# Half loads of A with a ScalarE copy, and B 0 by DMA: a change to a recommender tower in float32

## What is computed

```python
for W in Ws:                       # W0 (24*24, 64), W1 (24*64, 64), W2 (24*64, 64)
    H_prev = Xk.shape[1]
    Wr = W.reshape(F_, H_prev, W.shape[1])
    Xk = jnp.einsum('bfd,bhd,fho->bod', X0, Xk, Wr)
    outs.append(Xk.sum(axis=2))
...
h = jnp.concatenate([z, dense_ctx], axis=1)
h = jnp.maximum(h @ W_top1 + b_top1, 0.0)
h = jnp.maximum(h @ W_top2 + b_top2, 0.0)
y = h @ W_top3
```

## Time and profile before

| | us |
|---|---|
| median of 3 runs | 378.74 (377.19 to 379.49) |
| the profiled execution | 375.55 |
| its span, first to last instruction | 373.7 |
| TensorE busy | 353.9 (95%) |
| VectorE busy | 307.8 (82%) |
| ScalarE busy | 187.4 (50%) |
| GpSimd busy | 220.0 (59%) |
| mean granted TensorE clock | 0.991 |

### The profile page before, as it was taken

One profiled execution on the slowest core, in us unless ns is written; L12 is line 12 of the kernel. 1 busy time (PEld: TensorE's weight loads), 2 busy tenths in 40 slices (PEclk: granted clock), 3 DMA queues, 4 the chain that ended last, 5 costly groups with the idle time before them and its releaser, 6 DMA issues.

```text
span 373.7 us, 7214 instructions
## 1 busy us (share of the span) xinstructions
PE 353.9 (95%) x2754; PEld 160.2 (43%) x2754; DVE 307.8 (82%) x308; ACT 187.4 (50%) x352; POOL 220.0 (59%) x332
## 2 busy tenths in 40 slices
PE   0958999999999999999999999999999999999997
PEld 0736623322333345434343454444443444444475
DVE  2993399969897999979898999798999999997600
ACT  1112024146352667574747475837474676545564
POOL 5888888888887878888863888888840000000000
PEclk9978999999999999999999999999999999999999
DMA  7686998979989799989999799979996999540000
GB/s 205 217 160 147 230 165 193 231 166 214 232 196 247 149 232 257 247 178 226 237 241 247 171 254 264 256 147 248 270 251 139 239 257 257 145 139 0 3 2 2
DMA packets 56773, 71.55 MB, mean 191 GB/s; under 512 B 31041, under 2 KB 35777, under 8 KB 56738
## 3 DMA queue, kind: packets, MB, share of 16 engines
q1 hardware_dynamic: 49282, 69.56, 77.8%
q0 software_dynamic: 5376, 1.39, 3.6%
q10 hardware_dynamic: 2080, 0.13, 0.4%
HBM read 50.61 MB, written 1.58 MB: 140 GB/s over the span
## 4 chain that ended last, share of the span: by engine, by line
PE 88%; DVE 7%; ACT 2%; DMA 1%; issue 1%; SPq 0%; DVEq 0%; ACTq 0%
PE ps_x L436 55%; PE ps_b L436 10%; PE ps_tower L436 10%; PE ps_turn L436 7%; DVE Z L373 4%; PE ps_turn L492 3%; PE ps_tower L442 2%; PE ps_turn L500 2%; DMA small_ids_sb<-small_ids 1%; DVE Z L412 1%; ACT x_diag L729 1%; DVE small_ids_f L368 1%; DVE Z L402 1%; DVE x_diag L381 0%; ACT C L702 0%
## 5 line engine op out<-in xcount | busy, mean ns | idle before, releaser
L412 DVE TENSOR_TENSOR Z<-A,ps_b 128x1024 f32<-128x1024 f32 x192 | 221.0, 1213 | 9.8 <-PE ps_x L436 5.5
L230 POOL DMA_INDIRECT x_rows<-tbl,ids_sb x168 | 179.4, 1068 | 55.1 <-POOL pause_sb L241 30.6
L436 PE MATMUL ps_x<-Z,w_sb 128*64 128x512 f32 x768 | 184.2, 598 | 0.7 <-DVE Z L412 0.5
L436 PEld LDWEIGHTS ps_x<-Z,w_sb 128*64 128x64 f32 x768 | 49.3, 136 | 79.9 <-issue 56.1
L402 DVE TENSOR_TENSOR Z<-A,C 128x1024 f32<-128x1024 f32 x48 | 57.6, 1220 | 25.2 <-PE ps_x L436 8.8
L729 ACT ACTIVATE x_diag<-ps_turn,mask_sb 128x192 f32<-128x192 f32 x128 | 50.6, 607 | 14.6 <-PE ps_turn L500 14.6
L436 PE MATMUL ps_x<-Z,w0s_sb 128*64 128x512 f32 x192 | 45.2, 597 | 0.5 <-DVE Z L402 0.3
L241 POOL MEMSET pause_sb<- 128x144 f32 x160 | 40.4, 252 | 0.1
L712 ACT COPY ps_b<-B_sb 128x1024 f32<-128x1024 f32 x36 | 36.9, 1025 | 4.4 <-DMA B_sb<-x_sb 4.0
L742 ACT COPY G<-ps_turn 128x416 f32<-128x416 f32 x31 | 15.7, 505 | 46.7 <-PE ps_turn L436 45.6
L436 PEld LDWEIGHTS ps_turn<-x_diag,x_rows 128*64 128x64 f32 x496 | 25.2, 137 | 17.7 <-issue 17.7
(11 more groups left out here) (60 smaller groups left out, 184.9 us busy)
## 6 DMA issues: line engine op xcount, KB each, us to landing
A<-x_scratch SPq DMA_DIRECT2D x48, 512.0 KB, 11.9
B_sb<-x_sb SPq DMA_DIRECT2D x72, 256.0 KB
C<-x_scratch SPq DMA_DIRECT2D x32, 512.0 KB, 13.2
x_rows<-tbl,ids_sb POOLq DMA_INDIRECT x168
small_ids_sb<-small_ids SPq DMA_DIRECT2D x3, 512.0 KB, 6.1
x_quarters<-x_scratch SPq DMA_DIRECT2D x16, 96.0 KB
x_scratch<-x_rows SPq DMA_DIRECT2D x7, 192.0 KB
w_sb<-w SPq DMA_DIRECT2D x2, 384.0 KB, 5.2
```

The lines of the kernel that those rows point to most:

```text
L230: pool.indirect_dma_start(out=x0_rows[t % 2][:, f * D:(f + 1) * D], out_offset=None, in_=tables[f], in_offset=bass.IndirectOffsetOnAxis(ap ...
L412: nc.vector.tensor_tensor(Z[s % ZR][:, :], A[u % AS][i][:, :], ps_b[j % 2][:, :], ALU.mult)\
L436: return nc.tensor.matmul(out, lhsT, rhs, start=start, stop=stop)
```

## The change

From unit 4 on:

- A's loads write partitions 0 to 63 only (8 repeats instead of 16, 256 KB each), and a new copy_a on ScalarE copies each to partitions 64 to 127. copy_a(u+2) stands in slot u behind copy_c(u+2). It waits for the load and for the last reader of the set. cross1 waits for copy_a instead of the load.
- TensorE no longer makes B 0. SyncE spreads it from x1 (load_b0, two transfers of 256 KB, ahead of load_b) into B0_sb, a buffer that the first part of the kernel used for something else (small_ids_f32[0]), and VectorE reads it from there. B0_sb is single: the load waits until the three products of the unit before have read it.
- ps_b is now used by B 1, B 2 and B 3 alone, so copy_b's waits name other steps, which lie earlier. copy_x1 also waits for the B 0 load of the unit two before.

```diff
 def made_b(u, j):
-    return NJ * u + j + 1 if u < PB else NJ * PB + u - PB + 1
+    return NJ * u + j + 1 if u < PB else NJ * PB
...
+        B0_sb = small_ids_f32[0]
...
             def load_a(u, i):
-                sp.dma_start(A[u % AS][i][:, :], rows_of(u, FR * i, FR).to_broadcast([HR, FR, COLS]))\
+
+                times = HR if u < PB else HR // 2
+                sp.dma_start(A[u % AS][i][0:FR * times, :], rows_of(u, FR * i, FR).to_broadcast([times, FR, COLS]))\
                     .then_inc(A_in[u % AS][i], 16)
...
+            def load_b0(u):
+                sp.wait_ge(x1_copied, u + 1)
+                if u > PB:
+                    sp.wait_ge(z_ready, made_x2(u - 1, NI - 1))
+                for q in range(2):
+                    src = x1_sb[u % 2][H * q:H * (q + 1):NJ, :].unsqueeze(1)
+                    sp.dma_start(B0_sb[:, HALF * q:HALF * (q + 1)], src.to_broadcast([HR, FR, HALF])).then_inc(b0_in, 16)
...
                 if u > PB:
+                    load_b0(u - 1)
                     for k in range(NJ - 1):
                         load_b(u - 1, k)
...
             def cross1(u, i):
                 s = made_x1(u, i) - 1
-                dve.wait_ge(A_in[u % AS][i], 16 * (u // AS + 1))
+                if u < PB:
+                    dve.wait_ge(A_in[u % AS][i], 16 * (u // AS + 1))
+                else:
+                    dve.wait_ge(a_copied, NI * (u - PB) + i + 1)
...
-                nc.vector.tensor_tensor(Z[s % ZR][:, :], A[u % AS][i][:, :], ps_b[j % 2][:, :], ALU.mult)\
+                nc.vector.tensor_tensor(Z[s % ZR][:, :], A[u % AS][i][:, :],
+                                        B0_sb[:, :] if u >= PB and j == 0 else ps_b[j % 2][:, :], ALU.mult)\
                     .then_inc(z_ready, 1)
...
-                    if n == max(x1_at(u) + 1, 7) and u + 1 < UNITS:
+                    if n == max(x1_at(u) + 1, 7) and u + 1 < PB:
                         make_b(u + 1, 0)
...
                     act.wait_ge(b_made, made_b(u - 2, NJ - 1))
+                    if u - 2 >= PB:
+                        act.wait_ge(b0_in, 32 * (u - 2 - PB + 1))
...
+            def copy_a(u):
+                for i in range(NI):
+                    act.wait_ge(A_in[u % AS][i], 16 * (u // AS + 1))
+                    act.wait_ge(z_ready, made_x2(u - AS, NP2 - NI + i))
+                    nc.scalar.copy(A[u % AS][i][64:128, :], A[u % AS][i][0:64, :]).then_inc(a_copied, 1)
...
             def copy_b(u, k):
                 act.wait_ge(b_in[k], 32 * (u - PB + 1))
-                if k > 0:
+                if k == 2:
                     act.wait_ge(z_ready, made_x2(u, NI * k - 1))
                 else:
-                    act.wait_ge(z_ready, made_x2(u - 1, NP2 - 1))
+
+                    act.wait_ge(z_ready, made_x2(u - 1, NI * (4 - k) - 1))
...
                 if x1_at(u) == 0 and x1_at(u + 1) == 0 and u + 2 < UNITS:
                     copy_c(u + 2)
+                if PB <= u + 2 < UNITS:
+                    copy_a(u + 2)
```

More of the change, by code:

```diff
@@ L160, in cin_tower @@
         c2_in = sem("c2_in")
+        b0_in = sem("b0_in")
         b_in = [sem(f"b_in{k}") for k in range(NJ - 1)]
@@ L174, in cin_tower @@
         small_copied, small_ready = sem("small_copied"), sem("small_ready")
+        a_copied = sem("a_copied")
         c_copied, b_copied = sem("c_copied"), sem("b_copied")
@@ L350, in _ @@
                         sp.dma_start(dst, src).then_inc(tower_in, 16)
+            load_b0(UNITS - 1)
             for k in range(NJ - 1):
@@ L406, in cross2 @@
                 if i == 0:
-                    if u < PB or j == 0:
+                    if u < PB:
                         dve.wait_ge(b_made, made_b(u, j))
+                    elif j == 0:
+                        dve.wait_ge(b0_in, 32 * (u - PB + 1))
                     else:
```

## The result

The changed kernel takes 386.64 us (median of 4 runs, 384.86 to 389.47), the kernel before 378.98 us in the same session: a ratio of 1.0237, 95% interval 1.0184 to 1.029. It is slower, 7.7 us by the medians, where 389 was forecast. The profiled execution took 387.11 us, its span is 385.3 us against 373.7: 11.6 us more.

What follows compares the result with a forecast made beforehand. TensorE's and DMA's loops were taken as nearly tied. Unit 14's turn +8.3 us, slot 13 +0.7 and slot 14 -1.06 gave +7.9; with 2.2 for the clock, 10.1 on the median 378.74 made 388.8 us, range 376 to 398.

Steps and rivals of the forecast that it cites:

- TensorE's 1.06 us a slot: TensorE no longer runs make_b(u+1, 0): minus 1.06 us, twelve times, 12.7 us if nothing else held the end.
- VectorE at nothing: VectorE's 36 of 240 products reading B 0 from SBUF: 1220 ns against 1213, 0.25 us in all, counted as nothing.
- B 0 at 3.5 us a round: DMA: B 0 adds 512 KB a unit, 1.73 us, so 3.5 us per round of two units.
- Half loads as long as full ones: DMA: A's half loads still take 2.2 us on half the engines; relief 2.8 us a round, bounds 0 to 5.3.
- A of unit 14 4.5 us late: DMA: four rounds 0.7 us longer give 2.8, plus 1.73 for unit 4's B 0; A lands at 305.0.
- The chain from A to the turn, 7.8 us: ScalarE, unit 14: last copy 1.1 us after A lands at 305.0, copy_x2 6.7 later, x2's turn at 312.8.
- Slots with w = 1, +0.7: ScalarE: relu_h1(1) queued behind A's copies delays TensorE's sum_h1(2); slot 19.9 us against 19.2, 0.7 worse.
- The clock's 2.2 us and slot 13: TensorE: after 4.6 us idle before the turn, half clock loses 2.2 us (bounds 0 and 2.2); slot 13 adds 0.7.
- From the profiled run to the median: Whole kernel: the 10.1 us, found on the profiled run 3.2 us below the median, were added to 378.74.
- Half loads at half price: Rival, DMA: half loads relieve fully, A is in time, only ScalarE's chain remains; time 377 us, chance 0.18.
- No relief at all: Rival, DMA: round 43.1 us, unit 14's A 15.7 us late, 400 us; chance 0.10.
- TensorE's saving: Rival, TensorE: loads half price and ScalarE's copies fully in its gaps; up to -12.7, 366 us, chance 0.10.

Runs made afterwards that it cites:

- B 0 alone: Against the whole change: B 0 still spread by DMA, but A loaded whole into 128 partitions and copy_a gone; 392.86 us, ratio 1.0375 to the kernel before.
- half loads and copies alone: Against the whole change: all edits of B 0 undone, TensorE makes B 0, A's 256 KB loads and copy_a stay; 377.27 us, ratio 0.9994 to the kernel before.
- 16 rows: Whole change, but A's 256 KB loads read 16 rows, each repeated 4 times, outermost count 16 instead of 8; 377.47 us, ratio 1.0013 to the kernel before.

## Why the prediction was right, step by step

The direction and the path were right; of the causes behind them one was not, and part of the agreement in size is luck.

- *TensorE's 1.06 us a slot.* Right where nothing else holds the end: slot 14 fell from 17.4 to 16.3 us.
- *VectorE at nothing.* Right: 1220 ns.
- *B 0 at 3.5 us a round.* Right: 43.0 us with B 0 alone, 3.4 more than before. There the queue is full beyond the store, so bytes do set the round.
- *Half loads as long as full ones.* Right: with an outermost count of 16 the loss is gone. The relief that I took as 2.8 us a round measured 43.0 - 41.3 = 1.7, well inside the bounds 0 to 5.3 and below my value: half of the engines work little faster while the others rest.
- *A of unit 14 4.5 us late.* Mis-sized: about 6.9 (307.4 instead of 300.5). The step that failed is the addition, 1.73 once and 0.7 for each of four rounds. C of units 6, 8, 10, 12 and 14 was late by 0.4, 1.5, 4.3, 8.0 and 7.15 us (against 127.72, 167.48, 207.58, 246.63 and 286.15): 0.4 where I had 1.73, then 1.7 a round in place of 0.7, since the relief was 1.7 and not 2.8. Behind it is the sentence that nothing shortens the round from outside and that the loads' time sets it. GpSimd's gathers are a second bound that I hadn't seen: with half loads and copies alone the round falls by 0.8 us only and the store waits for them with DMA at 0.24. In the kernel before, loads and gathers were nearly tied. What the change cost was paid mostly at the store: 5.3 of the 7.15 us lie between its issue and C's.
- *The chain from A to the turn, 7.8 us.* Right: 7.7.
- *Slots with w = 1, +0.7.* Right in kind: 0.4 with half loads alone. In slot 13 of the change the wait for relu_h1(1) is 1.26 us.
- *The clock's 2.2 us and slot 13.* Together I had +2.9; slot 13 grew from 19.2 to 21.3 us, +2.1. The clock did fall to 0.50 behind the wait, of 3.52 us where I had 4.6.
- *Sum.* +10.1 against +11.6 of span: 2.4 more up to the turn at 315.18 (312.8 forecast), 0.8 less in slot 13.
- *From the profiled run to the median.* I added 10.1 to the median, as if the change would keep the 3.2 us by which the profiled run lay below it. It didn't: the changed kernel's profiled run (387.11) lies at its median, and the medians rose by 7.7, not by 11.6. The sum is 1.5 us short and this step 3.9 too much; that they nearly cancel, 389 against 386.64, is luck.

*The rivals.* Half loads at half price: not the case, but its price was well found. I gave 377 us for it, and the run that makes them so took 377.47, in part by luck: its slots with w = 0 were shorter than I had them, but C of unit 14 came late to ScalarE. No relief at all: nearly so in size, 1.7 of 13.2, yet 386.64 and not 400. With B 0 alone, where nothing is relieved, C of unit 14 does come 15.0 us late, where the rival has A 15.7, at 392.86 us. TensorE's saving: it had two obstacles that I gave, DMA and ScalarE, and a third that I had not seen. With both out of the way the time is 372.43, not 366; the rest I put down to the store behind the gathers and to the clock behind the waits, which no run takes away.

What stays open: whether loads or gathers set the round of the kernel before, since no run has faster gathers; the 5 to 7 us in which GpSimd stands idle between the first two gathers of tile 6 in every one of these kernels, for which the profile names no steady cause ("issue" in one, VectorE in another); and how much of the change's loss is the copies' own, since the run without them scattered.

## What to carry to other kernels

Halving a transfer's bytes need not halve its time; the half must still spread over all the engines: look at its outermost count, and at whether the end of a burst falls from full to idle or stays at half. When a loop's period looks like the sum of its transfers, ask also what its first step waits for; here one row of SyncE's waits, the store behind the gathers, would have led to an engine that is busy 59% of the time and still bounds the period. A cost that is paid in a round is free after the last round, so moving work to DMA for the last units alone kept a part of the gain that the whole change lost.

## What the runs showed of the hardware

- A transfer of 256 KB with outermost count 8 leaves the windows at a share of 0.55 to 0.59 and 136 to 163 GB/s; with count 16 into the same partitions they fall from 0.97 to 0.20 in 4 us.
- A small store (192 KB) behind a queue of loads holds C back, which waits for it, for 7.0 to 13.5 us in the change, where half of the engines have nothing to do at the end, and for 7.9 to 12.5 us with B 0 alone, where all are full; before for 3.9 to 8.0. With the queue idle (16 rows, 281.06 to 284.80) it is 3.7 us.
- GpSimd's gathers, mostly 0.95 us each, go out at one per 1.6 us on average (37.3 us for tile 7, 23 intervals). The store that waits for the last of them goes out 6.6 us behind it with DMA full (before), 4.5 us with DMA nearly idle (half loads and copies alone).
- Behind waits of TensorE of 3.52 and 3.88 us the granted clock was at 0.50, and eight matmuls took 3.53 us where four took 1.08 at full clock.
